# A decoder block on one core: in odd slots the next pair's first maximum is put ahead of the scaled probabilities, and transposes ahead of the values' products

## The reference

```python
x = attn(ln(x), ln(x), a1_*) + x      # 16 heads of 32, q, k, v quantised to 8 bits
x = attn(ln(x), context, a2_*) + x    # the same against a second input
a, g = split(ln(x) @ ff_w1 + ff_b1); x = a * gelu(g) @ ff_w2 + ff_b2 + x
x = x + attn8(ln(x), ln(ctx_1024))    # 8 heads of 64, no quantisation
```

```python
sim  = fq(q, dq, 128) @ fq(k, dk, 128).T * SCALE
attn = softmax(sim)
out  = fq(attn, dw, 0) @ fq(v, dv, 128)
return out @ wo + bo
```

## Time and profile before

| | us |
|---|---|
| median of 3 runs (lowest, highest) | 2745.76 (2745.1, 2751.56) |
| the profiled execution's own time | 2746.11 |
| its span, first to last instruction | 2744.3 |
| TensorE busy in the span | 2571.2 (94%) |
| VectorE busy | 1640.1 (60%) |
| ScalarE busy | 1417.0 (52%) |
| GpSimd busy | 676.4 (25%) |

### The profile page before, as it was taken

How to read it: one execution, slowest core, us unless ns; L and a number is a source line. 1 busy time by engine, 2 the same in 40 slices (tenths; PEclk the granted TensorE clock), 3 DMA queues, 4 the chain that set the end, 5 groups by cost and what they waited for, 6 DMA issues and landing times.

```text
span 2744.3 us, 54077 instructions
## 1 busy us (share of the span) xinstructions
PE 2571.2 (94%) x18304; PEld 2152.1 (78%) x18304; DVE 1640.1 (60%) x3945; ACT 1417.0 (52%) x3749; POOL 676.4 (25%) x1147
## 2 busy tenths in 40 slices
PE   5799999999999965999999999999999999999997
PEld 4566676677667643899999999999888888888885
DVE  6799999999999864634444343444443444444444
ACT  5688888888888862311111111122554555555554
POOL 1222222222222211223222222322222222222211
PEclk9899999999999987999999999999999999999998
DMA  4444444444444534311121112142111111111111
GB/s 152 91 96 96 95 93 101 98 95 92 93 100 91 97 63 134 118 67 71 53 80 57 69 61 76 61 148 68 43 58 38 53 50 49 46 46 53 46 38 39
DMA packets 335273, 211.06 MB, mean 77 GB/s; under 512 B 275568, under 2 KB 291952, under 8 KB 335216
## 3 DMA queue, kind: packets, MB, share of 16 engines
q1 hardware_dynamic: 335216, 210.34, 28.7%
HBM read 92.84 MB, written 50.33 MB: 52 GB/s over the span
## 4 chain that ended last, share of the span: by engine, by line
PE 56%; DVE 2%; issue 1%; ACT 1%; DMA 0%; POOL 0%; DVEq 0%; SPq 0%; POOLq 0%
PE AG L156 35%; PE Y L156 13%; PE XT L1295 3%; PE O L1318 2%; PE XT L1305 2%; PE XT L131 1%; DVE parts L1639 1%; DVE xhat L123 1%; PE Y L131 1%; PE O L1328 0%; DVE turned L185 0%; ACT stage L1535 0%; DMA stage<-in_ff_w_dram 0%; DVE mid_parts L1696 0%; POOL base L1851 0%
## 5 line engine op out<-in xcount | busy, mean ns | idle before, releaser
L156 PE MATMUL AG<-h_parts,up 128*128 128x256 f32 x6144 | 778.8, 285 | 13.4 <-DVE down L1620 10.1
L156 PEld LDWEIGHTS AG<-h_parts,up 128*128 128x128 f32 x6144 | 762.8, 193 | 25.9 <-issue 10.9
L594 ACT ACTIVATE e<-S,bias,qk_scale 128x256 f32<-128x256 f32 x1024 | 561.9, 570 | 122.8 <-POOL bias L793 122.8
L1503 ACT ACTIVATE gate<-AG,cols_pack 128x256 f32<-128x256 f32 x256 | 121.4, 474 | 669.5 <-PE AG L156 669.1
L1866 POOL TENSOR_TENSOR mid_parts<-mid_act,mid_parts 128x256 fp32r<-128x256 f32 x256 | 199.6, 780 | 1079.3 <-DVE mid_parts L1696 1079.3
L156 PE MATMUL Y<-down,mid_parts 128*128 128x512 f32 x1536 | 403.7, 400 | 0.0
L1689 DVE SCALAR_TENSOR_TENSOR mid_act<-AG,cols_pack,gate 128x256 f32<-128x256 f32 x256 | 123.4, 482 | 423.8 <-ACT gate L1503 422.8
L696 DVE TENSOR_REDUCE negmax<-S 128x4 f32<-128x1024 f32 x256 | 301.4, 1219 | 68.2 <-PE S L499 68.2
L156 PEld LDWEIGHTS Y<-down,mid_parts 128*128 128x128 f32 x1536 | 272.1, 189 | 68.5 <-issue 22.6
L714 DVE TENSOR_SCALAR pq<-e,rsum 128x256 uint16<-128x256 f32 x1024 | 292.5, 349 | 15.2 <-DMA pT<-pq 2.7
L147 PE MATMUL PJ<-w_a_wo,oT 128*128 128x512 f32 x512 | 238.9, 612 | 3.6 <-ACT oT L603 2.7
(11 more groups left out here) (125 smaller groups left out, 3466.6 us busy)
## 6 DMA issues: line engine op xcount, KB each, us to landing
stage<-in_ff_w_dram SPq DMA_DIRECT2D x48, 256.0 KB, 5.0
x_in<-in_x_dram SPq DMA_DIRECT2D x16, 512.0 KB, 3.9
ctx_in<-in_ctxT_dram SPq DMA_DIRECT2D x16, 512.0 KB, 3.5
mid_dram<-x SPq DMA_DIRECT2D x16, 512.0 KB, 2.7
own<-mid_dram SPq DMA_DIRECT2D x16, 512.0 KB, 3.3
own<-in_ctx_dram SPq DMA_DIRECT2D x16, 512.0 KB, 3.6
h_dram<-h3T SPq DMA_DIRECT2D x16, 512.0 KB, 2.6
k_dram<-own SPq DMA_DIRECT2D x16, 512.0 KB, 2.7
```

What stands on the lines that cost most here:

```text
L156: last = nc.tensor.matmul(acc, lhs(l), rhs(r), start=(start and i == 0), stop=(stop and i == 2))
L594: nc.scalar.activation(e[:, g % E_BUFS, i, :], S[g % 2][:, i // 2, i % 2, :], ACT.Exp, bias=bias[:, g % 2, i:i + 1], scale=qk_scale[:, ph. ...
L1503: nc.scalar.activation(gate[:, f % 2, :], AG[f % 2][:, TOK:2 * TOK], ACT.Gelu, bias=ff_b1[:, c:c + 1]).then_inc(gate_done, 1)
```

## The change

On TensorE a slot's transposes now come ahead of the values' products, and the other fills stay behind them. On VectorE, in odd slots, the first of the two maxima comes ahead of `dve_probs`, the second stays behind it. The exception is slot 7 of the phases P_B and P_Y (`early`), which keep the old order. On GpSimd, in the same odd slots, the long sums come behind the slot's `pool_dsum` and `pool_bias` and no longer ahead of them. No instruction is added, removed or resized.

```diff
--- before.py
+++ after.py
@@ -535,12 +535,17 @@
                             pe_scores(pe, ph, g + 1)
                         elif nxt:
                             pe_scores(pe, nxt, 0)
+                    for name, j in ph.steps(g):
+                        if kind_of(name) in TURNED:
+                            pe_fill(pe, at(ph.stage, ph.b, name, j))
+                    if g % 2:
                         if g >= 5:
                             pe_pv(pe, ph, g - 5)
                         elif prev:
                             pe_pv(pe, prev, g + GROUPS - 5)
                     for name, j in ph.steps(g):
-                        pe_fill(pe, at(ph.stage, ph.b, name, j))
+                        if kind_of(name) not in TURNED:
+                            pe_fill(pe, at(ph.stage, ph.b, name, j))
 
             def pe_drain(pe, ph):
 
@@ -739,19 +744,26 @@
                     wait_emptied(dve, (stage, b, "o1", j))
                 ln_stats(dve, ln, x1, m)
 
+            def max_ahead(ph, g, nxt):
+
+                return (g + 1 < GROUPS or nxt) and g % 2 and not (early(ph) and g == 7)
+
             def dve_phase(dve, ph, prev, nxt):
                 for g in range(GROUPS):
                     if ph is P_A:
                         for c in chunks_beside(g):
                             dve_weight_low(dve, c)
                     fills = [f for f in widened_beside(ph, prev, g) if kind_of(f[2]) in QUANTISED]
+                    into, m = (ph, g + 1) if g + 1 < GROUPS else (nxt, 0)
+                    ahead = max_ahead(ph, g, nxt)
+                    if ahead:
+                        dve_max(dve, into, m)
                     if g:
                         dve_probs(dve, ph, g - 1, fills)
                     elif prev:
                         dve_probs(dve, prev, GROUPS - 1, fills)
-                    into, m = (ph, g + 1) if g + 1 < GROUPS else (nxt, 0)
                     if g % 2 and into:
-                        for i in range(2):
+                        for i in range(1 if ahead else 0, 2):
                             dve_max(dve, into, m + i)
                     for where in transposed(ph, g, 1):
                         dve_transposed(dve, where)
@@ -824,24 +836,29 @@
                 nc.gpsimd.tensor_tensor(ctxT[:, 1, 0:2, :], ctx_in[:, 0:2, :], ctxT[:, 0, 0:2, :],
                                         ALU.subtract).then_inc(ctx_low_done, 1)
 
+            def pool_long(pool, ph, g):
+                if ph.ctx_at is not None and g == ph.ctx_at + 1:
+                    pool_beside_max(pool, ph, g)
+                    pool_ctx_low(pool, ph)
+                if ph.a == 1 and (ph.early or ("o1", 1) in ph.steps(5)) and g in (1, 3):
+                    pool_beside_max(pool, ph, g)
+                    pool_x1_bo(pool, ph.b, g // 2)
+                if ph.stage in ("loop", "peeled") and (ph.a, g) in ((1, 7), (0, 1)):
+                    half = 1 - ph.a
+                    wait_emptied(pool, (ph.stage, ph.b, "o1", half))
+                    pool_beside_max(pool, ph, g)
+                    pool_x_bo(pool, ph.b + 2, half)
+
             def pool_phase(pool, ph, nxt):
                 for g in range(GROUPS):
-                    if ph.ctx_at is not None and g == ph.ctx_at + 1:
-                        pool_beside_max(pool, ph, g)
-                        pool_ctx_low(pool, ph)
-                    if ph.a == 1 and (ph.early or ("o1", 1) in ph.steps(5)) and g in (1, 3):
-                        pool_beside_max(pool, ph, g)
-                        pool_x1_bo(pool, ph.b, g // 2)
+                    ahead = max_ahead(ph, g, nxt)
+                    if not ahead:
+                        pool_long(pool, ph, g)
                     if ph is P_Z and g in (6, 7):
                         pool_x1_bo(pool, ph.b, g - 6)
                     if ph is P_B and g in (5, 6):
                         wait_emptied(pool, ("first", 0, "o1", g - 5))
                         pool_x_bo(pool, 1, g - 5)
-                    if ph.stage in ("loop", "peeled") and (ph.a, g) in ((1, 7), (0, 1)):
-                        half = 1 - ph.a
-                        wait_emptied(pool, (ph.stage, ph.b, "o1", half))
-                        pool_beside_max(pool, ph, g)
-                        pool_x_bo(pool, ph.b + 2, half)
                     if g % 2:
                         pool_dsum(pool, ph, g)
                     if g + 1 < GROUPS:
```

## The result

The changed kernel takes 2818.11 us (2816.88 to 2819.45, 4 runs) against 2746.14 (2745.1 to 2751.56, 4 runs): 1.026 times as long, 95% interval 1.0247 to 1.0273. The prediction said 2808, range 2772 to 2826. The profiled executions differ by 2817.2 - 2744.3 = 72.9 us of span.

The account below looks back on a forecast made before the run. TensorE bounds the loop, VectorE just behind. 13 rounds at 4.3 us more make 55.9; with peeled round 3.1, last two phases 1.36 and 1.2, first two 0.9, together 62.5 on 2746.1: 2808 us, range 2772 to 2826.

Parts of the forecast that it names:

- T5: Slot 5 of a loop round's `two_` phase: values' fill starts late behind VectorE's residual, +1.00 us a round.
- U1: Slot 1 of a loop round's `one_` phase: fill behind VectorE's split comes late by the full block, +1.36 us.
- T7: Slot 7 of a loop round's `two_` phase: earlier first maximum brings the next scores sooner, -0.74 us a round.
- T1: Slot 1 of a loop round's `two_` phase: second group's exponentials start late, +0.54 us a round.
- The landings: In the loop, results awaited behind VectorE's second maximum come late: split +1.36 and +1.17 us, residual +1.00 and +0.99 a round.
- The starved group: Second group's exponentials, bias behind GpSimd's long sum, start at 4.35 us, not 3.81; +0.54 us a round at T1.
- rival (d): TensorE's clock falls in the loop: one or two fills a round about 1 us longer, 2821 to 2834; chance 0.06.
- The edges: Outside the loop: peeled round 3.1 us, last two phases +1.36 and 1.2, first two phases +0.9.
- (a): In the loop only the split lands late, residual delays are hidden: 2.3 us a round, 2780; chance 0.14.
- (b): No change: VectorE's 49.1 us of waiting in the loop swallow the moved block, 2746; chance 0.06.
- (c): Faster: T7's earlier maximum gains if results behind the second maximum have over 1.36 us spare, 2728; chance 0.08.
- (e): Whole kernel: scores and maxima keep their order and only names move; excluded by the code, no chance given.

## Why the prediction was right, and where it was off

**What bounds.** Right: TensorE's queue, with VectorE close behind, and in six of eight odd slots a maximum that couldn't come earlier. Of the signs named, the round came (64.43 of 64.7), the fills behind the split waited 1.25 and 1.72 us, and T5's values' fill started 4.27 us behind the first maximum (4.36 forecast); but its recorded wait is 0.27 and not about 1.0, scores wait 0.96 for exponentials at U1 and 0.61 at T3 (0.5 each forecast), and the first maximum's wait runs from none (T7) to 2.11 us (T1), not 1 to 2 everywhere.

**The landings.** Those of the split came within 0.03 us (1.36 and 1.17 forecast; 1.37 and 1.20). Those of the residual were taken as 1.00 and 0.99 and measured 0.63 and 0.62 at the next scores. The fill did start 0.92 us later (4.71 us after the scores; before 3.79, from T5's maximum at 447.16 less 0.43), but from its start to the next scores it took 2.96 us and no longer 3.24: behind an idle TensorE it is 0.28 us shorter than where it starts before the modelled end of another fill. (Its weight loads start with it in both, at 480.15 and 450.49.) Before, 0.56 us of the fill lay beside that other one, so a start 0.92 later isn't 0.92 lost. The forecast added a wait and left the fill as long as it was.

**T7.** Taken as -0.74, measured -0.38. The first maximum starts 0.62 us after the scores and not 0.43, since VectorE is late at T7 by its own work, and the second group's exponentials start 4.54 us behind it (483.74 to 488.28) and not 4.35. T5 and T7 together are the forecast's +0.26 (+0.25); that is in part luck.

**The starved group.** T1 was taken as +0.54, measured +0.68; the run with both maxima ahead took just that away. Mis-sized was the hand-over behind GpSimd's long sum: 0.3 us, rounded down from 0.40. In the changed kernel the bias follows the sum 4.01 us after the start of T1's first maximum (4.05 forecast; 2.58 + 0.23 + 1.29 of its own rows make 4.10), and the exponentials start 0.50 us after it, at 4.51 and not 4.35.

**The loop.** From the first fill of the first round to the one behind the last: 128.43 to 912.34 before, 135.45 to 975.31 after, 839.9 - 783.9 = 56.0 us; forecast 55.9. That the two agree so closely is luck: 13 typical rounds make 53.7, since the residuals were taken 0.74 us a round too dear and T7 and T1 together 0.50 too cheap, and 2.3 us lie in a few longer slots. Half of these is rival (d)'s mechanism: one fill behind the split's wait ran 1.15 us longer in the loop, and one just behind it 1.42,

```profile
780.33 4.29 PE L156 MATMUL PJ<-hT,w_a_wq 128*128 128x256 f32 x24 [1.72 <-DVE hT L690]
```

```profile
975.31 4.56 PE L156 MATMUL PJ<-hT,w_a_wq 128*128 128x256 f32 x24 [1.81 <-DVE hT L690]
```

with a granted clock of 0.57 beside the second, where the whole loop has 1.00 (with VectorE's and GpSimd's part alone neither fill is slow):

```profile
976.00:980.00 4.00, 4.00 (x29) 3.69 (x27) 0.62 (x3) 0.13 (x2) 0.00 (x0) 0.57 0.35 66
```

**The edges** are the step that failed: forecast 6.6, measured 72.9 - 56.0 = 16.9. Ahead of the loop it was 0.9 against 7.0. The step was: "What is moved on SP: the even group's transposing DMA is issued some microseconds later, for products five slots on; nothing." In the loop that holds: no engine has a recorded wait for a DMA there. In the first phase the loads of the next weights stand behind that DMA on SyncE's queue. SyncE before and after:

```profile
52.81 1.35 SPq L915 DMA_TRANSPOSE pT<-pq  x1
54.22 1.04 SPq L873 DMA_DIRECT2D x<-in_a_wq_dram  x2
```

```profile
55.57 1.35 SPq L934 DMA_TRANSPOSE pT<-pq  x1
56.98 1.05 SPq L892 DMA_DIRECT2D x<-in_a_wq_dram  x2
```

and ScalarE's cast of these weights, which stands ahead of the exponentials, before and after:

```profile
57.31 1.24 ACT L417 CAST w_a_wq<-x 128x512 fp32r<-128x512 f32 x2 [0.62 <-DMA x<-in_a_wq_dram]
```

```profile
60.01 1.21 ACT L417 CAST w_a_wq<-x 128x512 fp32r<-128x512 f32 x2 [3.28 <-DMA x<-in_a_wq_dram]
```

The load is issued 2.76 us later and the cast, waiting 3.28 us and no longer 0.62, starts 2.70 later. The run with the loads ahead bears this out for the first phase, where 3.8 of the 7.0 us lie. Another 1.1 is what was forecast as 0.9, 0.3 to 0.4 in each of three slots. The last 2.1 lie in P_B's slot 3: the output projection's fill took 8.80 us at a granted clock of 0.81, before 7.10 at 1.00. The loads ahead leave it at 8.49, and it took 9.04 in the run with the awaited results first and the old TensorE order, whose edges are the old ones; so it isn't the loads, and how much of it is the change stays open. Behind the loop it was 5.7 against 9.9 (72.9 - 56.0 - 7.0): the slow fill at 975.31 1.4, the rest of the peeled round 2.9 (3.1 forecast), the last two phases 4.3 (2.6 forecast), and 1.3 in the second half, which the change doesn't touch. I didn't take the last two phases apart.

**The rivals.** (a) falls: the residual's 26 waits. (b) and (c) fall by the time; (c)'s mechanism is real in T7, and alone it was worth 4 us. (d) had one or two slow fills a round and there were two in all, one of them just behind the loop. (e) falls: the scalings stand between the two maxima in VectorE's rows.

## What to carry to other kernels

Moving work on an in-order queue is priced by what stands behind it: find the results there that a full engine waits for and measure the slack of each, and follow the moved work's semaphores to the other queues, DMA issues included, also in phases that run once. An instruction that was waiting anyway wins nothing by standing further ahead; it turns its wait into everyone's. And a gain at one place must find room at the next: with both of T7's maxima ahead U1's scores came 1.3 us earlier, and VectorE, with a block more to do before U1's split, lost more than that.

## What the runs showed of the hardware

**Sums on GpSimd beside casts on VectorE.** A 128 x 512 cast from int8 took 1.49 us beside a long sum of GpSimd and 0.42 without; the long sum took 1.45 and 1.27. The Trainium skill, "SBUF — State Buffer", section "SBUF: two separate sides", says that the two engines share one pair of ports: of an instruction of GpSimd and one of VectorE that works in a 2-port mode or has two inputs in SBUF, the first to start holds the pair for its whole duration, and the other waits. The trace agrees: the cast ends 0.28 us after the sum, and its extra 1.07 us are most of one sum. In which mode VectorE works there no row tells.

**A clock that falls in some executions.** In the profiled execution with TensorE's part alone a wait of 1.35 us, scores, 0.28 us, transposes and 0.16 us came with a slow fill, and 10 of 14 slots U1 had one; the loop's granted clock was 0.98 and not 1.00. It costs about 1 us each time: the ten make most of the 11.4 us that this execution's span is longer. But these gaps alone don't do it. The two runs of the edges have the same code in the loop; one has five such slots, the one with the loads ahead none:

```profile
281.61 0.40 PE L499 MATMUL S<-kT,qT 32*128 32x256 bf16 x8 [1.34 <-ACT e L599]
282.28 1.14 PE L131 MATMUL PJ<-ident,xhat 128*128 128x128 f32 x8 [0.28 <-ACT q L567]
...
284.13 3.13 PE L156 MATMUL PJ<-ctxT,w_a_wk 128*128 128x256 f32 x24 [0.38 <-ACT turned L178]
```

What the profiled executions do show is that slow fills in the loop and the round behind it go with TensorE's new order: none in the three with the old one (kernel before, VectorE's and GpSimd's part alone, awaited results first), one to ten in nine of the eleven with the new one. The Trainium skill, "TensorE: Matmul & The Clock Gate", section "A second HAM failure mode: psum-queue depth-cycling", tells of another kernel whose clock swings because of frequent short idles between groups of matmuls. The run of TensorE's part alone agrees, with fills of 4.31 and 3.14 us; the run with the loads ahead doesn't, with almost the same idles and 3.13. What decides between them wasn't tried.
